# A gated convolution mixer computed on 40 instead of 52 diagonal columns per batch and block

## What is computed

```
B, HD, L = k.shape                     # k = v = ctx, q = layernorm(x); 16 heads of 8 channels, L = 256
kv = einsum('bhil,bhjl->bijhl', k_, v_)                    # per head: 8 x 8 products of channels
y = causal_convolution(kv, ssm_kernel)                     # along l, one kernel per head
out = y + kv * D
out = einsum('bijhl,bhil->bjhl', out, q_)                  # sum over i
x = x + tanh(g_xattn[0]) * out
```

## Time and profile before

| | us |
|---|---|
| median of 3 runs (lowest, highest) | 281.17 (281.05, 281.37) |
| the profiled execution, its own time | 282.44 |
| span of its trace | 280.7 |
| TensorE matmul busy | 250.0 (89%) |
| VectorE busy | 183.3 (65%) |
| ScalarE busy | 110.9 (40%) |
| GpSimd busy | 73.8 (26%) |
| mean granted clock of TensorE, share of full speed | 0.951 |

### The profile page before, as it was taken

The page is one execution under the profiler, slowest core; times in us unless marked ns, Lnnn a source line. Parts: engine busy times, 40 slices in busy tenths (PEclk is TensorE's granted clock), DMA queues, the critical chain, the costliest instruction groups (busy, mean ns, idle before and its releaser), DMA issues.

```text
span 280.7 us, 4752 instructions
## 1 busy us (share of the span) xinstructions
PE 250.0 (89%) x1656; PEld 236.1 (84%) x1656; DVE 183.3 (65%) x515; ACT 110.9 (40%) x229; POOL 73.8 (26%) x92
## 2 busy tenths in 40 slices
PE   7998699788789999899589798999999999986984
PEld 7997599778679988799589688999999999975783
DVE  2237989997896787866975267483474756675532
ACT  1400364560103341853535633561731671343321
POOL 1618685438685301000252201010011001102100
PEclk9999999999999999979979999999999999999555
DMA  5895435000000050000000000000010000101000
GB/s 156 247 243 206 131 108 175 0 5 0 1 2 0 2 183 4 0 4 0 0 2 0 2 0 1 4 0 2 0 37 2 0 2 1 37 2 37 1 21 19
DMA packets 14039, 11.51 MB, mean 41 GB/s; under 512 B 2912, under 2 KB 13760, under 8 KB 14016
## 3 DMA queue, kind: packets, MB, share of 16 engines
q1 hardware_dynamic: 13920, 11.16, 13.0%
q10 hardware_dynamic: 96, 0.05, 0.1%
HBM read 10.14 MB, written 1.07 MB: 40 GB/s over the span
## 4 chain that ended last, share of the span: by engine, by line
PE 38%; issue 37%; DVE 12%; POOL 8%; ACT 4%; DVEq 0%; POOLq 0%; ACTq 0%
PE bank L668 9%; PE bank L531 6%; PE bank L524 5%; PE bank L540 5%; POOL kv L1268 3%; PE bank L723 2%; PE bank L569 2%; POOL rstd L1246 2%; POOL fold L1279 2%; PE bank L737 2%; PE bank L571 2%; PE bank L570 2%; DVE prod L995 1%; PE bank L671 1%; DVE m_stack L1043 1%
## 5 line engine op out<-in xcount | busy, mean ns | idle before, releaser
L668 PE MATMUL bank<-w_split,xt 128*128 128x352 f32 x384 | 72.2, 339 | 0.0
L668 PEld LDWEIGHTS bank<-w_split,xt 128*128 128x128 f32 x384 | 63.7, 195 | 0.3
L1242 POOL TENSOR_SCALAR ve<-mv 128x2 f32<-128x2 f32 (+2 forms) x16 | 3.6, 226 | 151.2 <-DVE mv L954 151.2
L1161 DVE SCALAR_TENSOR_TENSOR act<-silu,scal,bank 128x176 f32<-128x176 f32 x64 | 22.6, 393 | 28.4 <-ACT silu L860 27.8
L524 PE MATMUL bank<-d_split,a_t 128*128 128x256 f32 x264 | 34.2, 286 | 1.7 <-DVE a_t L915 1.7
L860 ACT ACTIVATE silu<-bank 128x352 f32<-128x352 f32 x32 | 14.9, 464 | 50.8 <-PE bank L671 50.7
L524 PEld LDWEIGHTS bank<-d_split,a_t 128*128 128x128 f32 x264 | 32.3, 191 | 2.3 <-DVE a_t L915 2.2
L1279 POOL TENSOR_TENSOR fold<-prod 128x256 f32<-128x256 f32 x32 | 23.5, 743 | 22.4 <-DVE prod L998 22.1
L1268 POOL TENSOR_TENSOR kv<-ctx_ext 128x880 f32<-128x880 f32 x16 | 27.5, 1722 | 1.8 <-ACT ctx_ext L746 1.8
L569 PE MATMUL bank<-kv,toe 128*128 128x208 f32 x64 | 17.6, 356 | 6.9 <-DVE prod L998 3.3
L995 DVE TENSOR_TENSOR prod<-bank,q_ext 128x320 f32<-128x320 f32 x32 | 15.4, 483 | 8.0 <-PE bank L571 7.0
(11 more groups left out here) (136 smaller groups left out, 432.4 us busy)
## 6 DMA issues: line engine op xcount, KB each, us to landing
toe<-lag_rows SPq DMA_DIRECT2D x4, 512.0 KB, 6.0
ring<-in_down_p SPq DMA_DIRECT2D x2, 704.0 KB, 4.7
x_res<-in_x SPq DMA_DIRECT2D x2, 512.0 KB, 5.9
ctx<-in_ctx_rows SPq DMA_DIRECT2D x2, 512.0 KB, 5.9
ring<-in_gate_p SPq DMA_DIRECT2D x2, 512.0 KB, 5.4
ring<-in_up_p SPq DMA_DIRECT2D x2, 512.0 KB, 4.2
out_x<-x_res SPq DMA_DIRECT2D x3, 256.0 KB, 2.2
tern_w<-in_w_fc SPq DMA_DIRECT2D x1, 640.0 KB, 4.3
```

What stands on the lines that cost most here:

```text
L668: pe.matmul(psum((name, b, c))[:, 0:CW], lhs, w_split[:, w, kt, part, cols], start=i == 0, stop=False)
L1161: drain(dve.scalar_tensor_tensor(out=act[:, g * NI:(g + 1) * NI], in0=silu[:, n % 2, cols], scalar=scal[:, b, g:g + 1], in1=psum(("up", b, ...
```

## The change

Each diagonal is now computed for its 8 cyclic starts only: 5 x 8 = 40 columns in place of 52. Rows are extended only upwards (channels 0 to 7, then 0 to 3, EXT = 12), with two copies instead of three. Diagonals 3, 2, 1 can then no longer be read with a shift that wraps; VectorE writes them shifted to the right by 1 to 3 columns into rows of ROW = 11 columns of `prod`, so up to three terms for each batch and block lie in columns 8 to 10 and belong to columns 0 to 2. GpSimd adds these wrapped terms in a second, small add after its fold (3 x 3 elements for each of 8 batches and blocks, 72 for each partition), in place, and waits for its own first add before. What lies in columns 8 to 10 and is not written must be zero, so GpSimd clears both buffers of `prod` once at the start.

```diff
-SPAN = 11
-YW = TAPS * SPAN - 3
-EXT = 15
+YW = TAPS * HD
+EXT = HD + TAPS - 1
+ROW = HD + 3
...
-    reads = {"turn_ctx": 3, "turn_q": 3,
+    reads = {"turn_ctx": 2, "turn_q": 2,
...
-    kv = sb("kv", [P, 2, 4 * Q, TAPS, SPAN])
-    prod = sb("prod", [P, 2, 2 * Q, HD, HD])
+    kv = sb("kv", [P, 2, 4 * Q, TAPS, HD])
+    prod = sb("prod", [P, 2, 2 * Q, HD, ROW])
...
-        return [(...) for d0, s0, n in ((3, 0, 8), (0, 5, 3), (11, 0, 4))]
+        return [(...) for d0, s0, n in ((0, 0, HD), (HD, 0, EXT - HD))]
...
 # VectorE, conv
                     if hn >= 2:
                         dve.wait_ge(folded, hn - 1)
+                    else:
+                        dve.wait_ge(prod_cleared, 1)
-                    drain(dve.tensor_tensor(o[:, :, 0:TAPS, :], view(y, 0, [[YW, 2 * Q], [SPAN, TAPS], [1, HD]]),
-                                            view(q_ext, qb + 3, [[EXT, 2 * Q], [1, TAPS], [1, HD]]), ALU.mult), step)
-                    drain(dve.tensor_tensor(o[:, :, TAPS:HD, :], view(y, SPAN - 1, [[YW, 2 * Q], [SPAN - 1, 3], [1, HD]]),
-                                            view(q_ext, qb + 2, [[EXT, 2 * Q], [-1, 3], [1, HD]]), ALU.mult), step)
+                    drain(dve.tensor_tensor(o[:, :, 0:TAPS, 0:HD], view(y, 0, [[YW, 2 * Q], [HD, TAPS], [1, HD]]),
+                                            view(q_ext, qb, [[EXT, 2 * Q], [1, TAPS], [1, HD]]), ALU.mult), step)
+                    shifted_rows = view(prod, ((h % 2) * 2 * Q * HD + TAPS) * ROW + 1, [[HD * ROW, 2 * Q], [ROW + 1, 3], [1, HD]])
+                    drain(dve.tensor_tensor(shifted_rows, view(y, HD, [[YW, 2 * Q], [HD, 3], [1, HD]]),
+                                            view(q_ext, qb, [[EXT, 2 * Q], [0, 3], [1, HD]]), ALU.mult), step)
...
 # GpSimd, start
+            pool.memset(prod[:].rearrange("p a n s j -> p (a n s j)"), 0.0).then_inc(prod_cleared, 1)
 # GpSimd, kv
-                    pool.tensor_tensor(kv[:, n % 2], view(ctx_ext, base, [[EXT, 4 * Q], [0, TAPS], [1, SPAN]]),
-                                       view(ctx_ext, base, [[EXT, 4 * Q], [1, TAPS], [1, SPAN]]),
+                    pool.tensor_tensor(kv[:, n % 2], view(ctx_ext, base, [[EXT, 4 * Q], [0, TAPS], [1, HD]]),
+                                       view(ctx_ext, base, [[EXT, 4 * Q], [1, TAPS], [1, HD]]),
 # GpSimd, fold
-                    pool.tensor_tensor(f, p4[:, :, 0:4, :], p4[:, :, 4:8, :], ALU.add).then_inc(folded, 1)
+                    pool.tensor_tensor(f, p4[:, :, 0:4, 0:HD], p4[:, :, 4:8, 0:HD], ALU.add).then_inc(summed, 1)
+                    pool.wait_ge(summed, half * HEADS + h + 1)
+                    wrapped = f[:, :, 1:4, 0:ROW - HD]
+                    pool.tensor_tensor(wrapped, wrapped, p4[:, :, TAPS:HD, HD:ROW], ALU.add).then_inc(folded, 1)
```

More of the change, by code:

```diff
@@ L186, in use @@
         n_read[bank] += reads
-    reads = {"turn_ctx": 3, "turn_q": 3, "turn_router": 2, "turn_w": 2, "mask_up": 4, "turn_down": 2, "tern_sum": 1,
+    reads = {"turn_ctx": 2, "turn_q": 2, "turn_router": 2, "turn_w": 2, "mask_up": 4, "turn_down": 2, "tern_sum": 1,
              "turn_fc": 1, "turn_proj": 1, "turn_att": 1, "turn_x": 2, "logits": 2, "turn_top": 1, "flat": 3,
@@ L378, in build @@
     kv_made = sem("kv_made")
+    prod_cleared, summed = sem("prod_cleared"), sem("summed")
     folded, gathered = sem("folded"), sem("gathered")
@@ L448, in extended @@
                q_ext[:, :, t * Q:(t + 1) * Q, :]).rearrange("p h q e -> p q h e")
-        return [(dst[:, :, :, d0:d0 + n], src[:, :, :, s0:s0 + n]) for d0, s0, n in ((3, 0, 8), (0, 5, 3), (11, 0, 4))]
+        return [(dst[:, :, :, d0:d0 + n], src[:, :, :, s0:s0 + n]) for d0, s0, n in ((0, 0, HD), (HD, 0, EXT - HD))]
     def mixer_free(eng):
@@ L566, in pairs @@
                         return kv[:, g % 2, (2 * (h % 2) + t) * Q:(2 * (h % 2) + t + 1) * Q].rearrange(
-                            "p q d j -> p q (d j)")[:, :, 3:TAPS * SPAN]
+                            "p q d j -> p q (d j)")
                     y = psum(step)[:, 0:2 * Q * YW].rearrange("p (t q c) -> p t q c", t=2, q=Q)
@@ L697, in _ @@
                             last = pe.matmul(psum(step)[:, k * P:(k + 1) * P], qt[:, t, k * P:(k + 1) * P],
-                                             ctx_ext[:, half, :, t, q, 3:3 + HD], start=t == 0, stop=t == 1)
+                                             ctx_ext[:, half, :, t, q, 0:HD], start=t == 0, stop=t == 1)
                     fill(last, step)
```

## The result

The changed kernel takes **282.42 us** in the median of 19 runs (281.0 to 283.01), against 281.05 for the kernel before in the same comparison (19 runs). The ratio is **1.0043, 95% interval 1.0027 to 1.0059**. A second comparison gave 1.0036 (1.0019 to 1.0053). It is slower by about 0.4%, 1.2 us, where the forecast was no difference, 281.0; the time lies inside the range.

The account below looks back on a forecast made before the run. VectorE was taken to bound 28.9 to 64.4 us and TensorE 82.6 to 94.7. The terms +0.2 + 0.6 - 1.0 = -0.2 us, carried over to the median 281.17, gave 281.0 us, no difference; range 278.8 to 283.2.

Parts of the forecast that it names:

- TensorE, -1.0 from 82.6 to 94.7: Heads 12 to 15, where TensorE is full: 24 convolution instructions of 160 columns instead of 208 save 1.0 us.
- GpSimd's prices: Second add 0.45 us, wait 0.09, kv 1.35, fold 0.74 with +0.1 as upper end; a group +0.70 us.
- Start: Before the first convolution at 17.93 us: clearing prod, shorter copies and earlier kv change nothing; some 0.3 gain without cover.
- 17.9 to 64.4, +0.2: Mixer up to 64.4 us: head 4's constants held 0.7 us longer, mostly taken in; +0.2, ends -0.5 and +1.2.
- my sign for a right forecast: Among the signs of a right forecast: VectorE still full from 29 to 64 us.
- 64.4 to 82.6, +0.6: Second half's heads and first router: later kv delays logits 0.45 us, then held operations; +0.6, ends -0.5 and +1.8.
- held VectorE operations: Router's SBUF-to-SBUF operations, about 64.4 to 82.6 us, meet the longer GpSimd fold and are held: +0.4 us.
- Rival A: Thinner convolutions in the mixer let TensorE's clock fall once more: +0.8 to +2.0 us, about 282.3; chance 0.26.
- Rival B: The existing clock fall near 120 us goes away and its 1.46 us come back: 279.1 us; chance 0.21.
- Rival C: GpSimd becomes the bound, small add costing 0.74 us: +0.8 (28.9 to 64.4), +1.6 (64.4 to 82.6), 282.6 us; chance 0.13.
- the forecast alone: The main case, no difference at 281.0 us, without the rivals: 280.4 to 281.6 us; chance 0.28.

Follow-up runs that it names:

- the late add: Changed kernel with one 144-element wrapped add per group, placed behind the kv of the group two ahead, and four buffers of prod: 0.9965 of the kernel before.
- products in the gaps: 25 fp32 products that compute nothing, put where TensorE stood idle in the convolution stage: changed kernel 1.0041, kernel before 0.9988, both against the kernel before.

## Why the prediction was wrong, point by point

- **TensorE, -1.0 from 82.6 to 94.7.** Mis-sized: -0.45 to the fourth chunk in the chain. The 12 instructions between the first two chunks gave their 0.5; at heads 14 and 15 the chunk behind them waits for other engines. On the other hand the shorter products were worth more before the first chunk than I allowed: 52 columns on TensorE, all else as changed, cost 2.3 us in all, 0.7 of it before the first chunk (67.64 us from the first convolution, against 66.90) or 1.1 (against 66.53 without the fall).
- **GpSimd's prices.** Right: add 0.41 for 0.45, stop 0.07 for 0.09, kv 1.25 for 1.35, a group's new distance +0.6 for +0.70. The fold on rows of 11 took 0.04 more, inside its upper end.
- **Start.** Right in kind: nothing was seen of the clearing. The convolutions began 0.73 earlier, in a trace in which TensorE's products that compute nothing also got faster earlier (the first 23 of them take 4.03 us in the chain in place of 4.75).
- **17.9 to 64.4, +0.2.** This is the first step that failed, and its terms tell where. The prediction had the constants of head 4 held 0.7 us longer, and then let VectorE's idle time and ScalarE's shorter copies "take most of that in". They were held 0.65 longer (4.73 us against 4.08), and nothing took it in: +0.52 at the multiply of head 5, +0.70 at the second half. "From 28.9 VectorE ... sets the pace" was read from a busy share of 34.24 of 35.5 us. It held from 46.5 us on, where the chain takes 13.8 us with the adds and without them. Between 28.9 and 46.5 it did not: there the late add is 0.7 us faster than the changed kernel (17.1 against 17.8 us from `w_split` to `stats`), although its trace has a clock fall in that stretch. VectorE still reads 34.0 of 35.5 us, as my sign for a right forecast asked, so that sign could not tell.
- **64.4 to 82.6, +0.6.** The second step that failed: +1.5 in this trace, +1.1 in the one with products in the gaps (23.41 against 22.30). The first of it was right: the convolution behind group 2's kv 0.6 late, the logits 0.4 (forecast 0.45). "GpSimd then has a pause ..., so the delay does not grow" was nearly right too: without the fall the router's `gmax` at the last stage (L1138, 78.00) is 0.57 late. What was too small is the term for held VectorE operations, +0.4. In the trace without the fall it is 0.25 at the operation of L1111 (0.55 in place of 0.29), 0.6 at the operation that took 1.27 in place of 0.69, and 0.2 at the two behind it, 1.0 in all. In the changed kernel's own trace the second of these is not longer than before, and the fall stands in its place.
- **Held VectorE operations.** At 25.55 a scalar operation on 4 elements took 0.80 us beside kv, and L1111 took 0.53 in place of 0.29 in the second half. The Trainium skill (SBUF — State Buffer, Who interferes with whom) says that a VectorE instruction with two SBUF inputs contends with a GpSimd instruction that reads SBUF. The trace agrees for L1111, which runs from 71.55 to 72.08 while GpSimd's fold lasts until 71.94.
- **Rival A** happened in its mechanism and at its place (a fall at 74.1 us behind a thinner stretch), and over many executions: 29.4 us at the low clock against 27.2 on the same chip. Its price was 0.4 us for 6.8 us of fall in the one pair of traces that shows it, and some 1.1 for 10.2 us in another, at the low end of 0.8 to 2.0 or under it. Keeping the clock gained nothing that can be measured.
- **Rival B** did not happen. Both traces of the changed kernel have no fall at 120 us, but the stages ahead of it came later and not earlier, and the kernel before with products in the gaps has none there either.
- **Rival C** is the nearest to what was found, though at the forecast's prices and not at the upper ones: GpSimd's longer work costs in both stretches. I had tied it to an add of 0.74 us. Of its signs the first chunk after 84 came (84.10); waits for kv of over 5 us did not (3.9 us).

The sum was +0.2 + 0.6 - 1.0; the trace gives +0.7 + 1.5 - 0.45 = +1.75 up to the fourth chunk, and the runs +1.2 at the end. That the time lies inside the wide range says little for the working: it is outside the 280.4 to 281.6 that was given for the forecast alone, and all three terms were too favourable.

## What to carry to other kernels

Small operations added to an engine that is busy a quarter of the time can cost (here 4.7 us for 32 x (0.41 + 0.07) = 15.4 us of them), if they stand in a loop that several engines close by turns: add up the loop for one round, engine by engine, and compare it with the distance between rounds. Longer work on GpSimd also reaches VectorE without any semaphore, by the operations that it holds; if a held one lies on the chain, count it in full. A busy share of 95% is no proof of a bound where records overlap or hold waiting time; the chain's shorter durations are the ones to add up. And if a small fix-up has to go on a queue, put it behind what others wait for, with more buffers, rather than behind the operation that it fixes.

## What the runs showed of the hardware that I had not expected

- GpSimd's two-input operations lie within 0.1 us of one line: 72 elements 0.41 us, 144 elements 0.65, 256 elements 0.74 to 0.79, 640 elements 1.25, 880 elements 1.72. By a line through these, 0.3 to 0.4 us of it is fixed, so two adds of 72 (0.80 with their overlap) are not far from one of 144.
- The granted clock fell behind stretches in which TensorE was only moderately idle (1.63 of 3.4 us of records) and not behind others that read alike (1.64 of 3.4 us at 27.9 to 31.3 us). The two traces of the changed kernel show the same falls, but the mean granted clock of its 19 executions runs from 0.937 to 0.954.
- A fall of TensorE's clock of 6.8 us cost 0.4 us where VectorE's and GpSimd's work lay beside it, in one pair of traces; a fall of 3.4 us in front of dense products cost 1.46.
